# Expert result loads, a shared gating and a turn of maxima moved in a one-core FFN, attention, FFN kernel

## The chip, the cores and the metric

The kernel runs on one core of a Trainium2 chip, as one program. The metric is the device time of an execution in microseconds, and the median over several is compared. TensorE, VectorE, ScalarE, GpSimd and SyncE each run their own list of instructions in order and wait for one another through semaphores. SyncE only starts DMA transfers and waits.

## What is computed

Input are 4 sequences of 256 tokens with 512 features (float32), 1024 tokens in all. The core of the reference:

```python
x = L0_attn_hidden_states
x = x + 0.5 * _L0_ffn_ref(_layernorm(x), ...)   # router, 16 experts, shared expert
x = x + _L0_attn_ref(_layernorm(x), Wqkv, Wo)   # 32 query heads of 16, one key/value head, causal, ALiBi
x = x + 0.5 * _L0_ffn_ref(_layernorm(x), ...)   # same weights again
return x
```

The FFN sends each token to 2 of 16 experts (hidden size 128, chosen over 4 groups) and adds a shared expert (hidden size 256). An expert is `silu(x w1 + b1) * (x w2 + b2)`, then `w3`. Attention takes for each query head the softmax of scores plus a slope times the distance over the keys up to the query's own.

## The kernel before, in words

**Tiles.** The 1024 tokens are 8 tiles of 128 (`NT`), a tile on the 128 partitions. `x` stays in SBUF through all three parts. One large SBUF tensor, `arena`, is cut into named views that overlap in time. Thus `yg`, the gathered expert results of all tiles, lies over `xn` and `xnT`, the normalised tiles and their transposes: `yg[4]` to `yg[6]` lie over `xnT[0]` to `xnT[5]`, `yg[7]` over `xnT[6]` and `xnT[7]`. The views `pr`, `attn` and others of attention lie further behind.

**FFN** (`ffn_pe`, `ffn_act`, `ffn_dve`, `ffn_pool`, `ffn_sp`, called with f = 0 and f = 1). TensorE turns the tiles, does the router and the shared expert for tiles 0 to 5, then loops over 19 jobs (128 gathered token rows of one expert each). Results go to `y_dram` by scatters from GpSimd. Then come `shared_down(5)`, `shared_up(6)`, `shared_up(7)` (L1317, 16 matmuls each), and `shared_down(6)`. A `shared_down(t)` (L1358, two matmuls of 512 columns in float32, each of which the trace shows as two, and L1362, the bias matmul) waits for the gating of both tiles of its pair:

```python
pe.wait_ge(sem("s_h"), NT * f + 2 * (t // 2) + 2)
```

The gating `shared_h(t)` is one VectorE instruction (L856) behind ScalarE's silu (L632). `shared_x(t)` (L1004) adds a shared result to `x`; `pairs_x(t)` (L1014 and L1016) adds the two expert results of each token, once their load has landed.

**Loads of the expert results** (`ffn_sp`). Once all scatters have landed, SyncE issues `y_rows(range(4))`, in the first FFN the 1 MB of `wq` (into `wj`, L359), then waits for the last `shared_up` (`s_gu`) and issues `y_rows(range(4, NT))` (L355, 512 KB each), then waits for the last `shared_down` (`s_z`) and loads `wo`.

**The passage to attention** (`att_dve` L1203 and on, `att_pe`). VectorE's list is written out by hand: `pairs_x(0)`, `pairs_x(1)`, `att_stats(0)` (L1118 to L1122), `shared_h(7)`, `att_norm(0)` (L1131, two tiles, behind a reciprocal root on GpSimd, L552), `shared_x(6)`, `pairs_x(2)`, `shared_x(7)`, `pairs_x(3)`, `att_stats(1)`, and further pairs among the remainders of the q and k products (`rest`, L1150 and L1146). TensorE's list there: `shared_down(6)`, two turns of the normalised tiles (`xa_turn`, L1511), `shared_down(7)`, then the q and k products (L1522, L1530).

**Scores and maxima.** For each of 4 batches and 32 heads TensorE makes the scores (`scores`, L1551 to L1553) only to find each row's maximum; VectorE reduces them (`maxima`, L1159). The maxima are signed (`maxima_signed`, L1166 to L1168), turned by TensorE (`max_turn`, L1595), split in three bfloat16 parts by VectorE (`maxima_parts`, L1177 to L1180), written by SyncE to `m_dram` and read back as rows of `qside` (`m_rows`, L403 and L406), each for half of the heads. The scores of batch 0 are made among the q products of batches 2 and 3.

**The loop of attention.** 32 groups (4 batches of 8, q is the place in the batch). Group (b, q) holds four `scores` of batch b + 1, two `scores_t` of batch b (L1565, L1567, the turned scores with maxima), their exponentials on ScalarE (L762), a mask on GpSimd (L592), and `weigh` of the group before (L1579). The scores of batch b + 1 wait for VectorE to have reduced those two heads back. From head 16 on `scores_t` needs the second half of its batch's maxima, that is from group q = 4. For b = 1 to 3 the second turn of maxima stands inside group q = 0. For b = 0 it stands ahead of the loop: `maxima_signed(0, 1)` and `maxima_parts(0, 1)` at L1253 and L1254, `max_turn(0, 1)` at L1643, followed by a wait for the last `rest`.

Of the kernel before, what the change touches and what calls it, by code (L numbers as in the profile page):

```python
# [111 lines left out]
def build(nc, x_in, wqkv_in, wo_in, rw_in, rb_in, rbias_in, ew1, eb1, ew2, eb2, ew3, eb3,  # L112
          sw1, sb1, sw2, sb2, sw3, sb3, const_f, const_b, rows_q, rows_k, out):
    with ExitStack() as ctx:
# [5 lines left out]
        def sem(name):  # L120
            if name not in sems:
                sems[name] = ctx.enter_context(nc.semaphore(name))
            return sems[name]
# [203 lines left out]
        def ffn_sp(f):  # L327
            for t in range(NT):

                nc.sync.wait_ge(sem("xn"), NT * f + t + 1)  # L330
                nc.sync.dma_start(xn_dram[t * P:(t + 1) * P, :], xn[:, t, :]).then_inc(sem("xn_out"), 16)
            if f == 1:

                nc.sync.wait_ge(sem("a_wo"), NT)
                nc.sync.dma_start(sw3s, sw3.rearrange("(c p) d -> p c d", p=P)).then_inc(sem("wo_in"), 16)

            if f == 0:

                for e in range(0, E, EG):
                    for part in range(2):  # L340
                        if e > 0:
                            experts_in(nc.sync, e, part)
                    nc.sync.dma_start(w3[:, e:e + EG, :], ew3[e:e + EG].rearrange("e p d -> p e d")).then_inc(sem(f"ew_in{e // EG}"), 16)

            if f == 0:
                nc.sync.dma_start(wkv, wqkv_in[:, DIM:].rearrange("(c p) n -> p c n", p=P)).then_inc(sem("wqkv_in"), 16)
            nc.sync.wait_ge(sem("jex"), f + 1)
            rest = nc.sync.value_load(jm[:], min_val=JOBS_LEAST // 2 - AHEAD, max_val=JOBS // 2 - AHEAD)
            outs = nc.sync.to_reg(16 * rest + 32)
            nc.sync.wait_ge(sem(f"y_out{f}_1"), outs)  # L350
            nc.sync.wait_ge(sem(f"y_out{f}_0"), outs)
            nc.sync.wait_ge(sem("y_end"), 16 * (f + 1))
            def y_rows(tiles):
                for t in tiles:
                    nc.sync.dma_start(yg[:, t], y_dram.rearrange("(c n) d -> n c d", c=CHOICES)[t * P:(t + 1) * P]).then_inc(sem(f"yg{t}"), 16)  # L355

            y_rows(range(4))
            if f == 0:
                nc.sync.dma_start(wq, wqkv_in[:, 0:DIM].rearrange("(c p) n -> p c n", p=P)).then_inc(sem("wqkv_in"), 16)  # L359

            nc.sync.wait_ge(sem("s_gu"), NT * f + NT)
            y_rows(range(4, NT))
            if f == 0:
                nc.sync.wait_ge(sem("s_z"), NT)
                nc.sync.dma_start(wo, wo_in.rearrange("(c p) n -> p c n", p=P)).then_inc(sem("wo_in"), 16)
# [768 lines left out]
        def att_dve(pairs_x, shared_h, shared_x):  # L1134
# [27 lines left out]
            def maxima_signed(b, half):  # L1162

                hs = slice(half * HEADS // 2, (half + 1) * HEADS // 2)
                dve.wait_ge(sem("s_max"), HEADS * b + hs.stop)
                link(dve.tensor_tensor(m3[:, hs, 1], m3[:, hs, 1], m3[:, hs, 2], ALU.max))  # L1166
                dve.tensor_scalar(nm[:, 0, hs], m3[:, hs, 0], -1.0, None, ALU.mult)
                dve.tensor_scalar(nm[:, 1, hs], m3[:, hs, 1], -1.0, None, ALU.mult).then_inc(sem("m_nm"), 1)  # L1168

            def maxima_parts(b, half):  # L1170

                n = 2 * b + half
                dve.wait_ge(sem("m_t"), n + 1)
                if n >= 1:
                    dve.wait_ge(sem("m_out"), 32 * n)
                src = ps[0:QT * HEADS, m_bank(b, half), 0:P]
                link(dve.tensor_copy(mp[:, 0, :], src))  # L1177
                link(dve.tensor_tensor(mr[:], src, mp[:, 0, :], ALU.subtract))
                link(dve.tensor_copy(mp[:, 1, :], mr[:]))
                dve.tensor_tensor(mp[:, 2, :], mr[:], mp[:, 1, :], ALU.subtract).then_inc(sem("m_parts"), 1)  # L1180
# [20 lines left out]
                    dve.bn_stats(st[:, t, :], x[:, t, :]).then_inc(sem("stats"), 1)  # L1201

            pairs_x(0)  # L1203
            pairs_x(1)
            att_stats(0)
            shared_h(7)
            att_norm(0)
            shared_x(6)
            pairs_x(2)
# [28 lines left out]
            for b in (2, 3):  # L1238
                for n in range(len(ITEMS)):
# [10 lines left out]
                        values(b)  # L1250
                    if (b, n) == (3, 0):
                        maxima_signed(0, 0)
            maxima_signed(0, 1)  # L1253
            maxima_parts(0, 1)  # L1254
            for b in range(BATCH):
                more = b + 1 < BATCH
                for q in range(HEADS // 4):
                    n = 8 * b + q
                    if q == 0 and b >= 1:
                        maxima_signed(b, 1)  # L1260
                    if q == 4 and more:
                        maxima_signed(b + 1, 0)
                    if more:
                        maxima(b + 1, 4 * q, PS_S)
                        maxima(b + 1, 4 * q + 1, PS_S + 1)
                    if n >= 2:
                        normalise(n - 2)
                    if more:
                        maxima(b + 1, 4 * q + 2, PS_S)
                        maxima(b + 1, 4 * q + 3, PS_S + 1)  # L1270
                    if q == 0 and b >= 1:
                        maxima_parts(b, 1)
                    if q == 4 and more:
                        maxima_parts(b + 1, 0)
                    if q in (5, 6) and b >= 1:
                        residual(b - 1, q - 5)
                    if q == 7 and b >= 1:
                        row_stats(b - 1)
                        ln_stats(1, b - 1)
                    if b + 1 == BATCH and q in (2, 3, 4, 5):  # L1280
                        if q == 2:
                            dve.wait_ge(sem("st_done"), HEADS // 2 * b)
                        ln_rows(1, q - 2)
# [218 lines left out]
        def att_pe(shared_down):  # L1502
# [137 lines left out]
                if 1 <= b < BATCH - 1:  # L1640
                    xa_turn(b + 1, 1)
            pe.wait_ge(sem("v_in"), BATCH)
            max_turn(0, 1)  # L1643
            pe.wait_ge(sem("rest"), len(ITEMS) * BATCH)

            for b in range(BATCH):
                more = b + 1 < BATCH
                for q in range(HEADS // 4):
                    n = 8 * b + q
                    if (b, q) == (0, 0):  # L1650
                        pe.wait_ge(sem("rows1_in"), 16)
                    if (b, q) == (1, 1):
                        pe.wait_ge(sem("wo_in"), 16)
                    if (b, q) == (0, 0):
                        pe.wait_ge(sem("m_parts"), 1)
                    if more:
                        scores(b + 1, 4 * q, PS_S)
                    scores_t(b, 2 * q)
                    if more:
                        scores(b + 1, 4 * q + 1, PS_S + 1)  # L1660
                    if n >= 2:
                        if (b, q) == (0, 2):
                            pe.wait_ge(sem("m_parts"), 2)
                        if b >= 1 and q == 1:
                            pe.wait_ge(sem("m_parts"), 2 * b + 2)
                        if b >= 1 and q in (3, 4):
                            pe.wait_ge(sem("a_aT"), QT * (b - 1) + q - 2)
                        if more and q == 5:
                            pe.wait_ge(sem("m_parts"), 2 * b + 3)
                        if b >= 1 and q in (6, 7):  # L1670
                            pe.wait_ge(sem("att_x"), QT * (b - 1) + q - 5)
                        turn_back(n - 2)
                    if more:
                        scores(b + 1, 4 * q + 2, PS_S)
                    scores_t(b, 2 * q + 1)
                    if more:
                        scores(b + 1, 4 * q + 3, PS_S + 1)
                    if n == 1:
                        pe.wait_ge(sem("s_max"), HEADS)
                    if n >= 1:  # L1680
                        weigh(n - 1)
                    if q == 0 and b >= 1:
                        pe.wait_ge(sem("normed"), n - 1)
                        max_turn(b, 1)
                    if b >= 1 and q in (2, 3):
                        pe.wait_ge(sem("normed"), n - 1)
                        attn_turn(b - 1, q - 2)
                    if q == 4 and more:
                        if n >= 2:
                            pe.wait_ge(sem("normed"), n - 1)  # L1690
                        max_turn(b + 1, 0)
                    if b >= 1 and q in (5, 6):
                        pe.wait_ge(sem("normed"), n - 1)
                        out_product(b - 1, q - 5)
# [51 lines left out]
```

## Time and profile before

| | |
|---|---|
| median of 3 runs | 467.0 us (466.22 to 468.55) |
| the profiled execution | 467.78 us, span 466.0 us |
| mean granted TensorE clock | 0.97 |
| TensorE (matmul) busy | 409.6 us, 88% |
| VectorE busy | 261.9 us, 56% |
| ScalarE busy | 180.3 us, 39% |
| GpSimd busy | 162.7 us, 35% |
| first FFN, up to its last `shared_up` | 0 to 131 us |
| passage, q and k products | 131 to 201 us |
| loop of attention | 201 to 333 us |
| last FFN | 338 to 466 us |

The span runs from the first to the last instruction of the profiled execution; what lies around it is 1.8 us. Matmul time is modelled and pipelined, so neighbouring instructions overlap in the rows. The clock is a share of 2.4 GHz: 1.00 is that, 0.50 is 1.2 GHz, and a figure between is a stretch with both. "DVE" is VectorE, "ACT" ScalarE, "POOL" GpSimd, "SPq" SyncE's DMA issues. In a timeline row "[0.62 <-X]" says that the engine stood idle 0.62 us before, until X released it.

### The profile page before, as it was taken

The page shows a single profiled execution, that of the slowest core. Times are in us where ns is not written, and L with a number is a line of the kernel's source. Part 1 is how long each engine was busy: PE and PEld are TensorE (multiplying, and loading weights), DVE is VectorE, ACT ScalarE, POOL GpSimd, SP SyncE. Part 2 cuts the span into 40 slices and gives each one's busy share as a digit, 9 for nine tenths or more (in the row PEclk, how much of TensorE's full clock was granted, in tenths as well). Part 3 has the DMA queues.
Part 4 walks back from the last instruction along what each step waited for, and adds up shares of the span by engine and source line. Part 5 has one row for each costly group of instructions (what it writes and reads, how often), then busy time and mean ns, then how long its engine had stood idle before and what let it go on. Part 6 is the DMA issues. An engine that isn't in the chain of part 4 may idle for free.

```text
span 466.0 us, 8466 instructions
## 1 busy us (share of the span) xinstructions
PE 409.6 (88%) x2848; PEld 289.0 (62%) x2849; DVE 261.9 (56%) x729; ACT 180.3 (39%) x300; POOL 162.7 (35%) x230
## 2 busy tenths in 40 slices
PE   0799879999959979879999899798999879999982
PEld 1687567888636757546665465343687558888650
DVE  5489513333258955868885785633239932333347
ACT  1321235665102221146663364483522316665300
POOL 2611316665302852333332242252000054666300
PEclk9999998999979999979999999999999989999987
DMA  7999973534296479212211200020120042444277
GB/s 213 312 372 313 322 234 129 171 108 158 99 364 191 129 181 194 75 39 73 74 56 26 69 6 6 0 74 24 46 91 1 1 134 79 171 132 147 95 269 305
DMA packets 48620, 63.88 MB, mean 137 GB/s; under 512 B 7750, under 2 KB 28070, under 8 KB 48548
## 3 DMA queue, kind: packets, MB, share of 16 engines
q1 hardware_dynamic: 40220, 41.51, 28.2%
q0 software_dynamic: 6368, 19.19, 12.8%
q10 hardware_dynamic: 2000, 2.76, 2.0%
q8 instruction: 19, 0.31, 0.3%
q14 instruction: 13, 0.11, 0.1%
HBM read 46.06 MB, written 19.79 MB: 141 GB/s over the span
## 4 chain that ended last, share of the span: by engine, by line
PE 57%; DVE 15%; DMA 9%; SPq 9%; issue 5%; POOL 2%; ACT 1%; ACTq 0%; POOLq 0%; DVEq 0%
PE ps L1453 14%; PE ps L1460 7%; PE ps L1607 6%; SPq L320 5%; PE ps L1579 5%; PE ps L1438 3%; DMA w<-in_L_ffn_ew_dram 3%; PE ps L1317 3%; PE ps L1522 3%; PE ps L1551 3%; DMA q_dram<-arena 2%; DVE arena L1159 2%; PE ps L1553 2%; PE ps L1565 2%; PE ps L1589 2%
## 5 line engine op out<-in xcount | busy, mean ns | idle before, releaser
L1159 DVE TENSOR_REDUCE arena<-ps 128x3 f32<-128x384 f32 x128 | 67.2, 550 | 17.5 <-PE ps L1553 16.7
L1453 PE MATMUL ps<-arena,wj 128*128 128x128 f32 x608 | 75.5, 278 | 0.0
L1453 PEld LDWEIGHTS ps<-arena,wj 128*128 128x128 f32 x608 | 72.6, 195 | 1.0 <-issue 1.0
L762 ACT ACTIVATE arena<-ps 128x768 f32<-128x768 f32 x64 | 51.8, 811 | 50.7 <-PE ps L1567 49.8
L592 POOL TENSOR_SCALAR_AFFINE_SELECT arena<-arena 128x512 f32<-128x512 f32 x64 | 40.8, 637 | 83.3 <-ACT arena L762 82.9
L1056 DVE SCALAR_TENSOR_TENSOR arena<-ps,arena 128x128 f32<-128x128 f32 x38 | 13.3, 351 | 87.6 <-ACT arena L678 87.6
L1317 PE MATMUL ps<-arena,turns 128*128 128x256 f32 x256 | 57.6, 381 | 0.0
L1317 PEld LDWEIGHTS ps<-arena,turns 128*128 128x128 f32 x256 | 48.2, 190 | 8.1 <-issue 2.1
L524 POOL DMA_INDIRECT y_dram<-arena x38 | 38.4, 1011 | 40.1 <-DVE arena L1063 31.6
L519 POOL DMA_INDIRECT arena<-xn_dram,arena x34 | 33.2, 977 | 51.4 <-DVE arena L996 25.2
L1460 PE MATMUL ps<-w,arena 128*128 x76 | 40.1, 611 | 4.0 <-DVE arena L1056 4.0
L1551 PE MATMUL ps<-cb 128*128 128x256 bf16 x128 | 36.1, 282 | 5.0 <-DVE arena L1159 4.5
L1358 PE MATMUL ps<-turns,arena 128*128 128x512 f32 x64 | 33.7, 653 | 7.1 <-issue 7.1
L683 ACT COPY wj<-w 128x1024 f32 x38 | 39.6, 1047 | 0.0
L1553 PE MATMUL ps<-arena 116*128 116x256 bf16 x128 | 35.5, 278 | 0.0
L674 ACT COPY arena<-ps 128x512 f32<-128x512 f32 x38 | 22.3, 587 | 31.4 <-PE ps L1438 31.4
L1522 PE MATMUL ps<-arena,wj 128*128 128x256 f32 x128 | 31.6, 383 | 1.5 <-ACT arena L720 1.5
L632 ACT ACTIVATE arena<-ps,shb 128x256 f32<-128x256 f32 x16 | 7.6, 473 | 59.3 <-PE ps L1317 59.3
L1438 PEld LDWEIGHTS ps<-cf,arena 128*128 128x128 f32 x136 | 17.3, 145 | 20.3 <-issue 18.5
L1607 PE MATMUL ps<-turns,arena 128*128 128x512 f32 x64 | 29.5, 604 | 0.0
L1552 PE MATMUL ps<-arena 116*128 116x128 bf16 x128 | 28.8, 225 | 0.0
L1579 PE MATMUL ps<-arena 128*32 128x128 f32 (+1 forms) x512 | 27.8, 335 | 0.0
(190 smaller groups left out, 609.7 us busy)
## 6 DMA issues: line engine op xcount, KB each, us to landing
arena<-y_dram SPq DMA_DIRECT2D x16, 512.0 KB, 7.4
arena<-q_dram SPq DMA_DIRECT2D x36, 128.0 KB, 2.6
xn_dram<-arena SPq DMA_DIRECT2D x16, 256.0 KB, 5.8
w<-in_L_ffn_ew_dram SPq DMA_DIRECT2D x4, 1024.0 KB, 10.9
q_dram<-arena SPq DMA_DIRECT2D x16, 192.0 KB, 2.4
x<-_attn_hidden_states_dram SPq DMA_DIRECT2D x4, 512.0 KB, 6.0
out_dram<-x SPq DMA_DIRECT2D x8, 256.0 KB, 4.7
turns<-in_L_ffn_sw_dram ACTq DMA_DIRECT2D x3, 512.0 KB, 7.8
```

The source lines that it names most:

```text
L592: pool.affine_select(diagonal, diagonal, [[0, 2], [0, 2], [1, P]], ALU.is_ge, 0.0, base=0, channel_multiplier=-1).then_inc(sem("sel"), 1)
L683: act.copy(wj[:, par].rearrange("p c f -> p (c f)"), w12[:, ds(e, 1)].rearrange("p a c f -> p (a c f)")).then_inc(sem(f"wj{f}"), 1)
L762: act.activation(pr[:, n % 2, pair, :], ps[:, bank:bank + 2, :].rearrange("p a b -> p (a b)")[:, 0:768], ACT.Exp).then_inc(sem("exp"), 1)
L1159: dve.tensor_reduce(m3[:, h:h + 1, :], ps[:, bank, 0:3 * P].rearrange("p (n k) -> p n k", n=3), AX_X, ALU.max).then_inc(sem("s_max"), 1)
L1317: ins = pe.matmul(o, sw12[:, c, cols], xnT[:, 2 * pair:2 * pair + 2, c, :], start=(c == 0), stop=(c == KC - 1))
L1453: ins = pe.matmul(o, wj[:, par, c, n * INTER:(n + 1) * INTER], xgT[:, par, c, :], start=(c == 0), stop=(c == KC - 1))
L1460: pe.matmul(ps[:, PS_Y + par, :], hj[:, par, :], w3[:, ds(e, 1), :], start=True, stop=True).then_inc(sem(f"y{f}"), 1)
L1522: ins = pe.matmul(ps[:, PS_ST + c, 0:SEQ], wq[:, k, c * P:(c + 1) * P], xaT[b % 2][:, k, :], start=(k == 0), stop=(k == KC - 1))
L1551: pe.matmul(o.rearrange("p (n k) -> p n k", k=P)[:, 0:3:2, :], identb, mask, start=True, stop=True)
L1553: pe.matmul(o[:, P:3 * P], qside[0:R_MAX, p, h, P:2 * P], kT[0:R_MAX, b, :], start=False, stop=True, skip_group_check=True).then_inc(sem(" ...
L1579: ins = pe.matmul(o, vv[:, b, k, :], pr_blocks(n % 2, h // 2)[:, k * QT:(k + 1) * QT - k, h % 2, :], start=(k == 0), stop=True, skip_group ...
L1607: ins = pe.matmul(ps[:, at_bank(b, t), :], aT[t][:, c, :], wo[:, c, :], start=(c == 0), stop=(c == KC - 1))
```

## The change

Three edits. In `ffn_sp`, the loads of tiles 4 to 6 wait for the sixth `shared_up` (`s_gu` at `NT * f + NT - 2`) instead of the eighth, and only tile 7 waits for that; this holds in both FFNs. In `att_dve`, `shared_h(7)` stands ahead of `pairs_x(1)`. In the loop of attention the second turn of maxima of batch 0, with its signs and parts, stands inside group (0, 0), where the other batches have it; TensorE's wait for `normed` stays for b >= 1 alone.

```diff
--- before.py
+++ after.py
@@ -358,8 +358,10 @@
             if f == 0:
                 nc.sync.dma_start(wq, wqkv_in[:, 0:DIM].rearrange("(c p) n -> p c n", p=P)).then_inc(sem("wqkv_in"), 16)
 
+            nc.sync.wait_ge(sem("s_gu"), NT * f + NT - 2)
+            y_rows(range(4, NT - 1))
             nc.sync.wait_ge(sem("s_gu"), NT * f + NT)
-            y_rows(range(4, NT))
+            y_rows((NT - 1,))
             if f == 0:
                 nc.sync.wait_ge(sem("s_z"), NT)
                 nc.sync.dma_start(wo, wo_in.rearrange("(c p) n -> p c n", p=P)).then_inc(sem("wo_in"), 16)
@@ -1201,9 +1203,9 @@
                     dve.bn_stats(st[:, t, :], x[:, t, :]).then_inc(sem("stats"), 1)
 
             pairs_x(0)
+            shared_h(7)
             pairs_x(1)
             att_stats(0)
-            shared_h(7)
             att_norm(0)
             shared_x(6)
             pairs_x(2)
@@ -1250,13 +1252,11 @@
                         values(b)
                     if (b, n) == (3, 0):
                         maxima_signed(0, 0)
-            maxima_signed(0, 1)
-            maxima_parts(0, 1)
             for b in range(BATCH):
                 more = b + 1 < BATCH
                 for q in range(HEADS // 4):
                     n = 8 * b + q
-                    if q == 0 and b >= 1:
+                    if q == 0:
                         maxima_signed(b, 1)
                     if q == 4 and more:
                         maxima_signed(b + 1, 0)
@@ -1268,7 +1268,7 @@
                     if more:
                         maxima(b + 1, 4 * q + 2, PS_S)
                         maxima(b + 1, 4 * q + 3, PS_S + 1)
-                    if q == 0 and b >= 1:
+                    if q == 0:
                         maxima_parts(b, 1)
                     if q == 4 and more:
                         maxima_parts(b + 1, 0)
@@ -1640,7 +1640,6 @@
                 if 1 <= b < BATCH - 1:
                     xa_turn(b + 1, 1)
             pe.wait_ge(sem("v_in"), BATCH)
-            max_turn(0, 1)
             pe.wait_ge(sem("rest"), len(ITEMS) * BATCH)
 
             for b in range(BATCH):
@@ -1679,8 +1678,9 @@
                         pe.wait_ge(sem("s_max"), HEADS)
                     if n >= 1:
                         weigh(n - 1)
-                    if q == 0 and b >= 1:
-                        pe.wait_ge(sem("normed"), n - 1)
+                    if q == 0:
+                        if b >= 1:
+                            pe.wait_ge(sem("normed"), n - 1)
                         max_turn(b, 1)
                     if b >= 1 and q in (2, 3):
                         pe.wait_ge(sem("normed"), n - 1)
```

## Rows read from the trace of the kernel before

**Rows 1.** The page: granted TensorE clock in 40 slices, tenths.

```profile
PEclk9999998999979999979999999999999989999987
```

**Rows 2.** Chain that ended last, 120 to 235 us: start, us, what.

```profile
131.25 4.75 issue
136.00 3.75 PE ps L1358 x4
...
141.49 1.72 PE ps L1358 x4
```

**Rows 3.** Timeline, 128 to 144 us: start, us, engine line, [idle before <-releaser].

```profile
131.29 0.47 ACT L632 ACTIVATE arena<-ps,shb 128x256 f32<-128x256 f32 x1 [2.98 <-PE ps L1317]
132.16 0.75 DVE L1014 SCALAR_TENSOR_TENSOR x<-arena,hv,x 128x512 f32<-128x512 f32 x1 [0.62 <-DMA arena<-y_dram]
...
135.41 0.48 DVE L856 SCALAR_TENSOR_TENSOR arena<-ps,shb,arena 128x256 f32<-128x256 f32 x1
...
136.35 1.00 DVE L1131 TENSOR_SCALAR arena<-x,mv,rstd 128x512 f32<-128x512 f32 x2 [0.45 <-POOL rstd L552]
...
140.22 0.69 DVE L1004 SCALAR_TENSOR_TENSOR x<-ps,x 128x512 f32<-128x512 f32 x1 [2.87 <-PE ps L1362]
...
143.04 0.38 PE L1362 MATMUL ps<-e3x,arena 102*128 102x512 bf16 x1
...
143.46 0.69 DVE L1004 SCALAR_TENSOR_TENSOR x<-ps,x 128x512 f32<-128x512 f32 x1 [1.10 <-PE ps L1362]
```

**Rows 4.** Busy time by stretch: PE, PEld, DVE, ACT, POOL; PEclk, DMA share, GB/s.

```profile
134.00:135.00 1.00, 0.00 (x0) 0.00 (x0) 1.00 (x2) 0.00 (x0) 0.00 (x0) 0.55 0.99 338
...
140.00:141.00 1.00, 1.00 (x7) 1.00 (x6) 0.78 (x2) 0.00 (x0) 0.00 (x0) 0.53 1.04 385
...
143.50:160.00 16.50, 16.50 (x79) 12.23 (x78) 15.51 (x34) 4.55 (x12) 10.14 (x15) 1.00 0.50 141
```

**Rows 5.** Timeline, 199 to 203.3 us.

```profile
199.68 0.55 DVE L1159 TENSOR_REDUCE arena<-ps 128x3 f32<-128x384 f32 x1
...
200.92 0.16 DVE L1168 TENSOR_SCALAR arena<-arena 128x16 f32<-128x16 f32 x1
201.23 0.27 PE L1595 MATMUL ps<-cf,arena 128*64 128x128 f32 x1 [2.12 <-DVE arena L1168]
...
202.63 1.01 DVE L1159 TENSOR_REDUCE arena<-ps 128x3 f32<-128x384 f32 x2
...
203.23 0.40 PE L1551 MATMUL ps<-cb 128*128 128x256 bf16 x1 [0.73 <-DVE arena L1159]
```

**Rows 6.** Busy time by stretch, columns as in rows 4: start of attention.

```profile
203.00:209.00 6.00, 5.77 (x32) 3.56 (x36) 3.81 (x8) 2.59 (x4) 2.00 (x4) 0.50 0.06 11
209.50:212.50 3.00, 3.00 (x43) 1.91 (x36) 2.34 (x6) 1.99 (x3) 0.80 (x3) 1.00 0.00 0
```

**Rows 7.** Timeline of TensorE, 208 to 213 us.

```profile
208.46 1.19 PE L1579 MATMUL ps<-arena 128*32 128x256 f32 x16
```

**Rows 8.** DMA issues at 128.7 and 131.3 us: KB each, us to landing.

```profile
wj<-in_L_attn_Wqkv_dram SPq DMA_DIRECT2D x1, 1024.0 KB, 9.3
...
arena<-y_dram SPq DMA_DIRECT2D x1, 512.0 KB, 8.1
```

**Rows 9.** Last FFN: three stretches (columns as in rows 4), then the timeline.

```profile
450.00:451.00 1.00, 0.00 (x0) 0.00 (x0) 0.96 (x2) 0.00 (x0) 0.00 (x0) 1.00 0.98 375
452.00:453.00 1.00, 1.00 (x2) 0.48 (x3) 0.00 (x0) 0.00 (x0) 0.00 (x0) 0.50 0.64 166
453.50:463.00 9.50, 3.95 (x9) 1.34 (x7) 9.29 (x14) 0.00 (x0) 0.00 (x0) 0.86 0.96 367
...
453.24 0.75 DVE L1014 SCALAR_TENSOR_TENSOR x<-arena,hv,x 128x512 f32<-128x512 f32 x1 [1.59 <-DMA arena<-y_dram]
```

**Rows 10.** Timeline of SyncE, 200 to 216 us.

```profile
204.63 0.58 SPq L406 DMA_DIRECT2D arena<-m_dram  x2
214.44 1.87 SPq L389 DMA_DIRECT2D arena<-q_dram  x3
```

## The prediction

> **What bounds the kernel now.** I read the page first: TensorE's granted clock is near full except in a few of the 40 slices [rows 1]. One of these is the twelfth, 128 to 140 us, and the chain, read there in order of time, shows why: TensorE runs out of work at 131.25, stands for 4.75 us with nothing that the profile can name, and then does a shared down product (L1358, four matmuls) in 3.75 us, where the same four take 1.72 us a moment later [rows 2]. So that pause costs its length, and then a half-speed product.
>
> The timeline says what it waits for [rows 3]. `shared_down(6)` needs `shared_h(7)`. ScalarE has its input ready at 131.76 (131.29 + 0.47), but VectorE takes it in program order behind `pairs_x(1)` and `att_stats(0)`, at 135.41. TensorE starts 0.11 us after it ends (135.89 to 136.00). Then `shared_x(6)` waits 2.87 us for the product, and `shared_x(7)` comes at 143.46. From 143.5 to 160 VectorE is busy for 15.51 of 16.5 us [rows 4]: it bounds the stage that follows, and what it gains at 143.46 it keeps. The clock falls to 1.2 GHz (0.50) in 134 to 135, is there until shortly before 141 and then at 2.4 GHz (1.00) [rows 4].
>
> The same kind of place lies at the start of attention [rows 5]. VectorE's last maxima of the first batch begin at 199.68, `maxima_signed(0, 1)` ends at 201.08, and TensorE, without work since about 199.1, turns the maxima at 201.23, with 2.12 us of idle before it. Then VectorE splits them (201.50 to 202.63), and only then takes the first reduction of the next batch. TensorE has done two score products and waits for that: next matmul at 203.23. The clock is at 0.50 from 203 to 209; from 209.5 it is full [rows 6]. The first `weigh`, which closes group 1, ends at 209.65 [rows 7].
>
> **The loads (edit 1).** Tiles 4 to 6 of the expert results no longer wait for the last shared product. In the first FFN SyncE would issue them at 129.3 to 130.8 and not from 131.28; each issue is some 0.5 us. But the DMA engines are already full: their share is 0.99 at 134 to 135 and 1.04 at 140 to 141 [rows 4], the weights issued at 128.73 land only 9.3 us later, at 138.0, and tile 4, issued at 131.28, 8.1 us later, at 139.4 [rows 8]. The transfers land in the order of issue, one behind the other; a load put into the full queue sooner lands no sooner. Nor does one wait for it: `pairs_x(4)` is behind all of the work of rows 3. In the last FFN the queue is as full when tile 4 is issued (share 0.98 at 450 to 451), the wait that counts is the 1.59 us before `pairs_x(2)`, whose load isn't moved, and from 453.5 to 463 VectorE is busy for 9.29 of 9.5 us [rows 9]. I take 0. Bounds: a gain of 0.5 us, should the gap in the transfers at 452 to 453 (share 0.64 [rows 9]) come from the late issue; a loss of 0.5 us, should tile 7's issue stand one slot later. Past `wqkv`'s load nothing is moved, since the three loads come after it; its cover is 138.0 against the first q product at 143.4, and this shrinks to 2 us below.
>
> **`shared_h(7)` one place up (edit 2).** `pairs_x(0)` ends at 131.54 (132.16 less its idle of 0.62). `shared_h(7)` then runs at 131.8 to 132.28, mostly in the idle time before `pairs_x(1)`, which is pushed from 132.16 to 132.3: 0.14 us, carried through `att_stats(0)` to the reciprocal root on GpSimd, for which `att_norm(0)` waits [rows 3]. Before, `shared_h(7)` lay under that wait (0.45 us of it are left in the row), so it cost VectorE nothing there; now the cover is the wait for a load, and if this went it would cost up to its 0.48 us. `att_norm(0)` begins at 136.49 instead of 136.35, its two halves done at 137.0 and 137.5. TensorE starts `shared_down(6)` at 132.39 and, still at full clock, needs 2.1 us (1.72 for the four matmuls [rows 2] and 0.38 for the bias [rows 3]), to 134.5. Then it waits for `att_norm(0)` up to 137.1. What is next late is thus this normalisation. Upper bound of the gain: at full clock the two turns end at 137.9 and `shared_down(7)` at 140.0, `shared_x(7)` stands at 140.05, 3.4 us early. Lower bound: clock at half from 137: two turns to 138.4 (1.3 us, from 140.2 to 141.49, where the next product began [rows 2, 3]), the down product with its bias 4.2 us as from 136.00 to 140.2, where `shared_x(6)` began [rows 3], `shared_x(7)` at 142.6, 0.9 us early. Here stands an idle time of 2.6 us after 2.1 us of work. The nearest row is the other pause: 2.12 us after dense work, and the clock was down within 1.8 us of its end [rows 5, 6]. So I expect a fall, but a late one that takes a part of the stage: the middle, **2.2 us**.
>
> The Trainium skill (TensorE: Matmul & The Clock Gate, Part 1, on oscillation) lets the clock fall only after a pause longer than 2.12 or 2.6 us. This trace doesn't agree: its fall at 203 follows a pause of 2.12 us [rows 5, 6]. By the rule the clock would hold in this stage, and the term be the upper bound, 3.4 us.
>
> **The second turn of maxima (edit 3).** Nothing is removed: one transpose, three instructions of signs and four of parts all stay. TensorE's first scores of the next batch no longer stand behind the turn. They need the last maxima (199.68 + 0.55), so they start at 200.35, not 201.46: 1.1 us. VectorE goes from the signs (201.08) straight to the reductions of group 0, a pair each 1.01 us [rows 5]: 201.1 to 203.3 with a small wait for the scores; the parts follow, 1.1 us, to 204.4; then four more, of which the second lets the last score product of group 1 go: 205.45, and `weigh(0)` runs 205.9 to 206.7. Before, group 1 ended at 209.65, 2.95 us later; I take **2.8 us** if the clock holds. 0.5 us of it is the wait for the turn that is now hidden, the rest the half speed that is not paid and the place of the parts behind group 0's products. TensorE's pauses are then 1.25 us and a few under 1.4 us, shorter than each pause after which the rows show a fall. If the clock falls all the same, 1.1 us (the earlier start) is left. The wait that moves is TensorE's for `maxima_signed`: behind it stood all of group 0, now group 1's scores, when it has long been met. The maxima's own round trip through memory is later by 1.8 us; its second half was issued at 204.63, its reader is a product of group 4 at about 215.4 (209.65 and two groups of 2.9), and SyncE's next work starts at 214.44 [rows 10]: hidden, with a cover of some 7 us.
>
> **Sum.** The profiled execution took 467.78 us, 0.8 above the median of 467.0. 467.78 less 2.2, 2.8 and 0 is 462.8. Some runs at the median may have lost less to the clock and then have less to win, so I don't take the 0.8 off as well: **462.9 us**, and the rivals stand against 467.78 too. What a measurement can tell from no change is about 0.5%, 2.3 us; faster means under 464.7.
>
> **Rivals.** A is the forecast, 0.46.
>
> B: the clock holds at both places. 467.78 less 3.4 and 2.8: 461.6 us. For it: no pause above 2.6 us is left there. Against it: the fall after 2.12 us. 0.14. The skill's rule quoted above comes out here.
>
> C: the first gain is absorbed. The start of attention is paced by something that edit 2 doesn't move, such as the weights' landing at 138.0 or the round trip of q through memory. Against it: VectorE's 15.51 of 16.5 us behind it. Only 2.8 is left: 465.0. 0.15.
>
> D: the clock falls again in groups 0 and 1. 2.2 and 1.1 us off: 464.5. 0.13.
>
> E, slower: the parts now stand between groups 0 and 1, so that TensorE pauses for some 1.3 us at 203.7 to 205, and the fall comes not in groups paced by VectorE but in the dense ones, 2 and later (3.00 of 3.00 us busy at 209.5 to 212.5 [rows 6]), where each us at half clock costs half a us. The spells at half clock here last near 7 us [rows 4, 6]; two of them cost 6.8 us. Less the 2.8 and the least of edit 2, 0.9, that is 3.1 slower: 470.9. It decides once more than 7.4 us behind 205 run at half clock. 0.06.
>
> F: neither stall is on the way to the end, and the time is 467.0. Against it: the chain runs through both. 0.06.
>
> **How the numbers follow.** Range: from B's time less 1.4, for runs that lie 0.8 lower as the median did and loads that gain 0.5, to C's and 0.6 for loads that lose: 460.2 to 465.6. Outside are E, F and tails. Faster: nearly all of A, B, half of D, a quarter of C: 0.70. Slower: E, 0.06. The same: 0.24.
>
> **What would show it.** Edit 2: no idle of 4.75 us before L1358 but one near 1.1, and one of 2.6 before L1511; `shared_x(7)` at 140 to 142.5. If it is at 143, edit 2 failed. Edit 3: L1595 behind four score products, the second group of `weigh` ending some 7.6 us after the last maxima of batch 0 and not 9.9; clock at 1.00 there. Edit 1: tile 4 lands at 139.4 all the same, with a longer time from issue to landing. Wrong would be: a stage behind 160 us that gives the early start back, or half clock in groups 2 to 4.

## The result, and the profile after

The changed kernel takes 463.68 us (median of 20 runs, 458.89 to 465.42), the kernel before 467.55 us (median of 20 runs of the same comparison). The ratio is 0.9922, with a 95% interval of 0.99 to 0.9945: clear of 1, and under 1%. Each ratio here is the comparison's own and not the quotient of the medians; the two can differ by 0.3% (edit 2 alone, below: 0.9918, and 0.9949 from the medians). One execution of the kernel before in the last of the comparisons below, of 2291.56 us, was in a slower state and is in no ratio. The forecast was 462.9 us, in a range of 460.2 to 465.6. The profiled execution took 463.63 us, against 467.78 us before.

The page of the changed kernel, for [rows 1] and the table:

```profile
span 461.9 us, 8466 instructions
PE 411.6 (89%) x2848; PEld 289.2 (63%) x2849; DVE 260.0 (56%) x729; ACT 180.6 (39%) x300; POOL 163.5 (35%) x230
...
PEclk9999998999998989999999999999999979999997
```

Busy time has hardly moved, the clock row has. From here on, lines of the file behind `ffn_sp` and before L1253 are two higher in the changed kernel (the gating is L858, `shared_x` L1006, `pairs_x` L1016 and L1018, the maxima L1161); those of TensorE are as before.

The passage, timeline of the changed kernel, for [rows 3]:

```profile
131.79 0.48 DVE L858 SCALAR_TENSOR_TENSOR arena<-ps,shb,arena 128x256 f32<-128x256 f32 x1
...
132.37 1.96 PE L1358 MATMUL ps<-turns,arena 128*128 128x512 f32 x4 [1.13 <-issue]
...
137.06 1.07 PE L1511 MATMUL ps<-cf,arena 128*128 128x128 f32 x8 [2.52 <-DVE arena L1133]
...
137.97 3.38 PE L1358 MATMUL ps<-turns,arena 128*128 128x512 f32 x4
...
141.80 0.69 DVE L1006 SCALAR_TENSOR_TENSOR x<-ps,x 128x512 f32<-128x512 f32 x1 [2.38 <-PE ps L1362]
```

`shared_h(7)` runs at 131.79, TensorE is idle for 1.13 us and not 4.75, and the pause has moved: 2.52 us now stand before the turn of the normalised tiles. `shared_down(7)` takes 3.38 us for its four matmuls, which is half speed, and `shared_x(7)` starts at 141.80, 1.66 us before that of [rows 3].

Busy time by stretch in the changed kernel (columns as in [rows 4]):

```profile
134.00:135.00 1.00, 0.55 (x2) 0.00 (x0) 1.00 (x2) 0.00 (x0) 0.00 (x0) 1.00 0.99 350
138.30:141.50 3.20, 3.20 (x5) 1.16 (x4) 1.09 (x2) 0.51 (x2) 0.00 (x0) 0.50 1.05 390
165.60:168.80 3.20, 3.20 (x14) 2.20 (x12) 0.56 (x1) 0.37 (x1) 0.82 (x2) 0.50 0.79 183
199.00:205.00 6.00, 4.82 (x50) 2.85 (x49) 5.38 (x14) 3.33 (x5) 2.36 (x5) 1.00 0.14 40
298.70:302.00 3.30, 3.30 (x30) 1.35 (x23) 1.15 (x3) 2.28 (x4) 1.94 (x3) 0.50 0.06 11
```

The clock now holds at 134 to 135, where it had fallen [rows 4], but falls at about 138, in the passage; again at 165.5, at 298.6, and later in the last FFN. At 199 to 205, the place of [rows 6], it is full.

The start of attention, for [rows 5] and [rows 7]:

```profile
197.83 0.55 DVE L1161 TENSOR_REDUCE arena<-ps 128x3 f32<-128x384 f32 x1
...
198.63 0.27 PE L1551 MATMUL ps<-cb 128*128 128x256 bf16 x1 [1.36 <-DVE arena L1161]
...
199.16 2.25 DVE L1161 TENSOR_REDUCE arena<-ps 128x3 f32<-128x384 f32 x4
...
201.33 0.27 DVE L1179 CAST arena<-ps 64x128 bf16<-64x128 f32 x1
...
203.01 0.28 PE L1551 MATMUL ps<-cb 128*128 128x256 bf16 x1 [1.09 <-DVE arena L1161]
...
204.00 0.86 PE L1579 MATMUL ps<-arena 128*32 128x256 f32 x16
```

From the start of the last maxima to the end of the first `weigh` it took 9.97 us before (199.68 to 209.65) and takes 7.03 now (197.83 to 204.86). TensorE starts the scores after 1.36 us of idle, VectorE does four reductions in a row, then the parts (L1179), and TensorE's wait for the reduction behind them is the 1.09 us at 203.01.

To see where the time went, each instruction of the new trace is set against its twin, the same instruction in the old one. The new kernel is ahead by

| at (us of the trace before) | ahead by | what changed there |
|---|---|---|
| 143.5, `shared_x(7)` | 1.66 | edit 2 |
| 170 to 184 (TensorE) | 0.02 | half clock from 165.5, which the old execution didn't have |
| 199.7, last maxima of batch 0 | 1.85 | the store of q that both wait for landed 1.8 us sooner |
| 209.7, end of the first `weigh` | 4.8 | edit 3 |
| 306 to 370 | 3.5 | half clock from 298.6 |
| 442, last scatter | 3.2 | half clock once more at 370 |
| 466, end | 4.1 | tile 2 landed sooner behind the last scatter |

The third line of this table is a wait of ScalarE for a store of q, in the timeline of the changed kernel and then in that of the kernel before:

```profile
184.66 0.37 ACT L738 CAST arena<-ps 128x256 bf16<-128x256 f32 x1 [2.81 <-DMA q_dram<-arena]
```

```profile
186.50 0.87 ACT L736 CAST arena<-ps 128x256 bf16<-128x256 f32 x2 [4.64 <-DMA q_dram<-arena]
```

The stores were issued by SyncE at these times, in the same order:

```profile
178.52 1.26 SPq L381 DMA_DIRECT2D q_dram<-arena  x2
```

```profile
180.52 1.29 SPq L379 DMA_DIRECT2D q_dram<-arena  x2
```

So the lead of edit 2 wasn't lost at 165.5. TensorE lost it there, but SyncE kept it: its store of q is issued 2.0 us sooner and lands 6.1 us later instead of 5.9, and behind that wait the other engines have the lead back. The half clock at 165.5 cost nothing at the last maxima.

### The profile page after: what moved, and what is told of

It is laid out like the page before. It is cut to its first block, busy times and chain, and to the rows that moved or that the text cites. A ratio compares the mean times of both kernels' runs of the same rounds, so it can differ in the third digit from the quotient of the medians.

```text
span 461.9 us, 8466 instructions
## 1 busy us (share of the span) xinstructions
PE 411.6 (89%) x2848; PEld 289.2 (63%) x2849; DVE 260.0 (56%) x729; ACT 180.6 (39%) x300; POOL 163.5 (35%) x230
## 4 chain that ended last, share of the span: by engine, by line
PE 59%; DVE 17%; SPq 8%; DMA 8%; issue 4%; POOL 2%; ACT 1%; ACTq 0%; POOLq 0%; DVEq 0%
PE ps L1453 14%; PE ps L1460 7%; PE ps L1607 6%; SPq L320 5%; PE ps L1579 5%; PE ps L1522 4%; PE ps L1438 3%; DMA w<-in_L_ffn_ew_dram 3%; PE ps L1551 3%; PE ps L1317 3%; DVE arena L1161 2%; PE ps L1553 2%; PE ps L1565 2%; PE ps L1589 2%; SPq L343 2%
## 5 line engine op out<-in xcount | busy, mean ns | idle before, releaser
L1161 DVE TENSOR_REDUCE arena<-ps 128x3 f32<-128x384 f32 x128 | 67.3, 551 | 16.9 <-PE ps L1553 15.9
L1453 PE MATMUL ps<-arena,wj 128*128 128x128 f32 x608 | 76.5, 280 | 0.0
L1453 PEld LDWEIGHTS ps<-arena,wj 128*128 128x128 f32 x608 | 73.6, 197 | 1.0 <-issue 1.0
L1358 PE MATMUL ps<-turns,arena 128*128 128x512 f32 x64 | 34.9, 674 | 3.5 <-issue 3.5
L1522 PE MATMUL ps<-arena,wj 128*128 128x256 f32 x128 | 32.7, 393 | 1.5 <-ACT arena L722 1.5
L1607 PE MATMUL ps<-turns,arena 128*128 128x512 f32 x64 | 29.5, 604 | 0.0
```

Of the source, the lines that this page charges most:

```text
L1161: dve.tensor_reduce(m3[:, h:h + 1, :], ps[:, bank, 0:3 * P].rearrange("p (n k) -> p n k", n=3), AX_X, ALU.max).then_inc(sem("s_max"), 1)
L1453: ins = pe.matmul(o, wj[:, par, c, n * INTER:(n + 1) * INTER], xgT[:, par, c, :], start=(c == 0), stop=(c == KC - 1))
L1522: ins = pe.matmul(ps[:, PS_ST + c, 0:SEQ], wq[:, k, c * P:(c + 1) * P], xaT[b % 2][:, k, :], start=(k == 0), stop=(k == KC - 1))
L1607: ins = pe.matmul(ps[:, at_bank(b, t), :], aT[t][:, c, :], wo[:, c, :], start=(c == 0), stop=(c == KC - 1))
```

## The experiments

Eleven runs were made, of ten kernels (the changed one again among them), each timed beside the kernel before on its chip. They fall into three comparisons, and the kernel before had medians of 466.74, 466.44 and 467.66 us in them; a ratio is always to the one of its own comparison.

### Each edit alone

**Edit 1 alone** (the diff of `ffn_sp`).

> The kernel before with edit 1 alone (tiles 4 to 6 of the expert results issued behind the sixth shared up product). My theory: the DMA engines are full, the loads land one behind the other in the order of issue, so tile 4 lands at 139.4 to 140.3 in the first FFN as before though issued 2 us sooner, and the time is that of before within 0.5 us, 467 to 468. Rival: the profile of the changed kernel ended 1.1 us sooner behind its last scatter (22.9 us against 23.9) because of this edit; then this run is 0.7 to 1.1 us faster than before, and its last scatter to end is near 22.9.

467.83 us; ratio 1.0014 (0.9984 to 1.0044). Tile 4 in the first FFN was issued at 127.5, and its row of the DMA issues (KB, us to landing) is

```profile
arena<-y_dram SPq DMA_DIRECT2D x1, 512.0 KB, 10.4
```

so it landed at 137.9, 15.7 us behind the last scatter's start at 122.2. Before, that was 139.4 less 124.0, 15.4 us. Issued 2 us sooner, landed no sooner, as in a full queue. Over all profiles it is 14.7 to 16.7 us in the six without edit 1 and 15.1 to 16.4 in the seven with it. The rival's short end, 23.0 us from last scatter to the end, did come (461.9 less 439.0 is 22.9 in the changed kernel). But two kernels without edit 1, edit 3 alone and the kernel before with a filled pause (below), ended after 23.0 and 22.9 us too. The long end of the profile before, 23.9, was tile 2, which landed late in that execution.

**Edit 2 alone** (the diff of `att_dve`'s first list).

> The kernel before with edit 2 alone (shared_h(7) ahead of pairs_x(1)). My theory: the pause of 4.75 us before shared_down(6) becomes 1.1 us, shared_x(7) starts at 140.1 to 142.6 (143.46 before), and what is won there, 0.9 to 3.4 us, reaches the end: 464.1 to 466.6, the likeliest 465.4. Rival: the gain is absorbed between 160 and 200 us by the round trips of q through memory; then the last maxima of batch 0 start at 199.7 as before and the time is that of before within 0.5 us.

464.36 us; ratio 0.9918 (0.9885 to 0.9951). Timeline:

```profile
132.20 1.96 PE L1358 MATMUL ps<-turns,arena 128*128 128x512 f32 x4 [1.13 <-issue]
...
136.89 1.06 PE L1511 MATMUL ps<-cf,arena 128*128 128x128 f32 x8 [2.52 <-DVE arena L1131]
...
137.79 1.88 PE L1358 MATMUL ps<-turns,arena 128*128 128x512 f32 x4
...
139.93 0.69 DVE L1004 SCALAR_TENSOR_TENSOR x<-ps,x 128x512 f32<-128x512 f32 x1 [0.68 <-PE ps L1362]
```

Here the clock held over the same pause of 2.52 us, `shared_down(7)` took 1.88 us, and `shared_x(7)` began at 139.93. Measured from the last scatter of the first FFN that is 3.4 us sooner than before (16.1 us behind it, against 19.5), the upper bound of the prediction; in the changed kernel it was 1.66. Busy time by stretch of the same run:

```profile
134.00:138.00 4.00, 1.48 (x11) 1.13 (x10) 3.08 (x9) 0.45 (x1) 0.72 (x1) 1.00 1.04 391
163.00:168.00 5.00, 4.92 (x16) 3.58 (x17) 0.60 (x3) 0.40 (x2) 1.72 (x4) 0.50 0.75 175
201.00:206.00 5.00, 5.00 (x24) 3.13 (x24) 3.12 (x6) 1.85 (x3) 1.88 (x3) 0.50 0.05 10
```

The clock then fell in the next stage, at 163 to 168, and again at 201 to 206, since the turn is still in its old place: of the 3.5 us ahead at 160, TensorE had 0.3 left at 175 and 2.3 at the last maxima. SyncE was still 3.0 us ahead at 180. So the rival of a full absorption falls, and that of a partial one has something to it, by way of the clock and of the wait for q.

**Edit 3 alone** (the diff of the loop and of L1253, L1254, L1643).

> The kernel before with edit 3 alone (the second turn of maxima of batch 0 in group 0). My theory: from the start of the last maxima of batch 0 to the end of the first weigh it takes 7.0 to 7.7 us and not 10.0, with the clock at 1.00, and the median is 2 to 2.8 us under before, 464.7 to 465.5. Rival: without edit 2 the clock still falls there in most executions, since the pause of 1.3 us remains; then 8.5 to 9 us, and about 1 us under before.

464.21 us; ratio 0.9945 (0.992 to 0.9971).

```profile
200.38 0.55 DVE L1159 TENSOR_REDUCE arena<-ps 128x3 f32<-128x384 f32 x1
...
205.56 0.28 PE L1549 MATMUL ps<-cb 128*128 128x256 bf16 x1 [1.09 <-DVE arena L1159]
...
206.55 0.86 PE L1577 MATMUL ps<-arena 128*32 128x256 f32 x16
```

200.38 to 207.41 is 7.03 us, as in the whole change, at full clock, without edit 2 (TensorE's lines are two lower in this kernel: L1549 is the scores, L1577 `weigh`). In all six profiles of kernels that have edit 3 as written, this interval was 7.02 or 7.03 us. Its rival is out.

**Edits 2 and 3 without edit 1**, run twice, the second time beside the whole change.

> Edits 2 and 3 without edit 1. My theory: edit 1 is worth nothing, so this is as fast as the whole change, 3.5 to 4 us under before: 463.5 to 464.1. Rival: edit 1 is worth about 1 us at the end of the last FFN; then 464.6 to 465.

> Edits 2 and 3 without edit 1, again, for the comparison with the whole change on one chip. Theory: equal to it or up to 0.8 us slower, with a wait before pairs_x(4) of the last FFN. Rival: about 1 us faster than the whole change.

> The changed kernel again, all three edits, beside the next run on the same chip. Theory: edit 1 is worth 0 to 0.8 us, since in the last FFN VectorE takes tile 4 right behind tile 3 here, while with the late issue it waited 0.5 to 0.85 us for it in three profiles of four. Then this is 0 to 0.8 us faster than edits 2 and 3 without it. Rival, from the first comparisons (0.9922 against 0.9896 of before, on different chips): edit 1 costs about 1 us; then it is slower by that.

462.09 us, ratio 0.9896 (0.9862 to 0.9929) at first; then 465.37 us, 0.9949 (0.9916 to 0.9982), beside 464.43 us, 0.9949 (0.9914 to 0.9984) of the whole change. Edit 1 can't be told from nothing in the time.

The profile of the whole change run again differs from the first one in the passage:

```profile
137.05 1.06 PE L1511 MATMUL ps<-cf,arena 128*128 128x128 f32 x8 [2.52 <-DVE arena L1133]
...
137.95 1.88 PE L1358 MATMUL ps<-turns,arena 128*128 128x512 f32 x4
```

The pause is the same 2.52 us, and the clock held behind it.

In the last FFN the trace shows something, though. In the first of the runs without it, tile 4 was issued at 446.08, and VectorE waited for it:

```profile
arena<-y_dram SPq DMA_DIRECT2D x1, 512.0 KB, 6.4
```

```profile
450.21 0.75 DVE L1014 SCALAR_TENSOR_TENSOR x<-arena,hv,x 128x512 f32<-128x512 f32 x1
...
452.52 0.75 DVE L1014 SCALAR_TENSOR_TENSOR x<-arena,hv,x 128x512 f32<-128x512 f32 x1 [0.77 <-DMA arena<-y_dram]
```

In the changed kernel it was issued at 443.72:

```profile
arena<-y_dram SPq DMA_DIRECT2D x1, 512.0 KB, 7.9
```

It landed 12.7 us behind the last scatter's start (443.72 + 7.9 less 438.95), against 13.7 us in the run without (446.08 + 6.4 less 438.78). The wait for tile 4, 0.77 us here, was 0.59 in edit 2 alone and 0.38 in the filled pause; there was none in the kernel before, in edit 3 alone and in the second run of edits 2 and 3 (three waits in six profiles, not the three in four that the expectation counted). In none of the seven profiles with edit 1 does VectorE wait for tile 4. But the landings of tile 4 overlap, 12.4 to 13.6 us behind the last scatter's start with edit 1 and 12.6 to 13.7 without, and so do the ends, 22.6 to 24.5 us behind it with edit 1 and 22.8 to 23.9 without. So a wait goes in some executions, and a sooner end is not shown.

### Is edit 3's gain the clock, or the order?

The kernel before, with TensorE kept at work in the pause:

```diff
             pe.wait_ge(sem("v_in"), BATCH)
+            for _ in range(16):
+                pe.matmul(ps[:, PS_A, 2 * P:4 * P], identb, cb[:, 0:2 * P], start=True, stop=True)
             max_turn(0, 1)
```

> The kernel before with 16 matmuls of 256 columns in bfloat16 (never read, some 1.8 us) in the pause of 2.12 us before the second turn of maxima; nothing else changed, so the order of the work stays. Theory 1, the gain of edit 3 is the clock: last maxima to the end of the first weigh takes about 7.5 us instead of 10.0, and the median is 1.5 to 2.3 us under before. Theory 2, the gain is the order (TensorE's earlier start and the hidden turn): the interval stays above 9 us, and the time is within 0.7 us of before.

464.88 us; ratio 0.9971 (0.9948 to 0.9994).

```profile
197.98 0.55 DVE L1159 TENSOR_REDUCE arena<-ps 128x3 f32<-128x384 f32 x1
...
199.44 0.30 PE L1595 MATMUL ps<-cf,arena 128*64 128x128 f32 x1 [0.28 <-DVE arena L1168]
...
204.66 0.86 PE L1579 MATMUL ps<-arena 128*32 128x256 f32 x16
```

```profile
200.00:205.50 5.50, 4.63 (x47) 2.61 (x46) 5.01 (x12) 3.25 (x4) 2.05 (x4) 1.00 0.18 48
```

The order is the old one, the turn still waits for the signs, yet the interval is 197.98 to 205.52, 7.54 us. Of the 2.94 us that edit 3 takes off the profile, 2.43 are the half clock that isn't there, and 0.51 the order. Theory 1 holds for the interval. The median gains less, 1.6 us, than the 2.4 of the profile; the profile of edit 1 alone shows why: its old order took 8.44 us there, since its spell at half clock was half as long. The pause doesn't cost every execution the same. In the time of all executions the filling brought about half of what edit 3 alone did (0.9971 against 0.9945, intervals that overlap), not four fifths.

### Is the loss in the passage the clock?

The changed kernel with TensorE at work in the moved pause:

```diff
             pe.wait_ge(sem("s_x"), NT - 2)
+            for _ in range(5):
+                pe.matmul(ps[:, PS_GU, 0:2 * P], sw12[:, 0, 0:P], sw12[:, 0, 0:2 * P], start=True, stop=True)
```

> The changed kernel with five matmuls of 256 columns in float32 (results never read, some 2.2 us) on TensorE between shared_down(6) and the turn of the normalised tiles, where it stands idle 2.52 us. My theory: the pause is what lets the clock fall to 0.50 at about 138 in the profile of the changed kernel; with it filled, shared_down(7) takes 1.9 us and not 3.4, shared_x(7) starts at 140.1 instead of 141.8, and the median is about 1.2 to 1.7 us under the changed kernel (462 to 462.5). Rival: the loss of clock there isn't on the way to the end, or comes from elsewhere; then shared_x(7) may be early but the time is that of the changed kernel within 0.5 us, or 0.2 us more for the added work.

461.94 us; ratio 0.9902 (0.9868 to 0.9936).

```profile
134.02 2.32 PE L1506 MATMUL ps<-turns 128*128 128x256 f32 x10
136.61 1.11 PE L1513 MATMUL ps<-cf,arena 128*128 128x128 f32 x8 [0.27 <-DVE arena L1133]
...
137.56 1.88 PE L1358 MATMUL ps<-turns,arena 128*128 128x512 f32 x4
...
139.69 0.69 DVE L1006 SCALAR_TENSOR_TENSOR x<-ps,x 128x512 f32<-128x512 f32 x1 [0.64 <-PE ps L1362]
```

```profile
134.00:141.00 7.00, 6.74 (x31) 4.81 (x30) 5.41 (x12) 1.07 (x2) 0.72 (x1) 1.00 1.03 388
185.20:188.20 3.00, 3.00 (x11) 1.06 (x9) 2.04 (x7) 0.00 (x0) 1.06 (x2) 0.50 0.00 0
```

The five matmuls (L1506 here, the turn is L1513) end 0.27 us before the turn is released. `shared_down(7)` takes 1.88 us, `shared_x(7)` begins at 139.69, 16.1 us behind the last scatter's start (17.8 in the changed kernel). So the half speed there was the pause's doing, and that part of the rival is out. Whether the gain reaches the end is less clear: the clock is at 0.50 at 185.2 to 188.2 instead, behind the wait for q, and the lead over the kernel before shrinks from 4.4 us at 180 to 2.8 at the last maxima. The ratio is lower than that of the whole change in both of its comparisons, but the intervals overlap.

### The parts one group on

```diff
-                    if q == 0:
+                    if q == (1 if b == 0 else 0):
                         maxima_parts(b, 1)
```

> The changed kernel with maxima_parts(0, 1) behind the maxima of group 1 instead of group 0. My theory: TensorE's wait of 1.09 us inside group 1 goes (it stood behind the parts), the first weigh ends about 6.0 us after the start of the last maxima instead of 7.0, of which the turning back in group 2 gives a part back, as it waits for the parts: 0.3 to 0.9 us under the changed kernel. Rival: VectorE paces these groups, so all of it comes back in group 2, and the time is that of the changed kernel within 0.3 us.

462.30 us; ratio 0.9905 (0.9871 to 0.9939).

```profile
198.46 0.55 DVE L1161 TENSOR_REDUCE arena<-ps 128x3 f32<-128x384 f32 x1
...
203.58 0.86 PE L1579 MATMUL ps<-arena 128*32 128x256 f32 x16
...
206.83 0.86 PE L1579 MATMUL ps<-arena 128*32 128x256 f32 x16
```

The first `weigh` ends 5.98 us after the start of the last maxima (198.46 to 204.44), 1.05 us sooner than in the changed kernel. The second ends after 9.23 us instead of 9.91, so 0.37 of the 1.05 is given back in group 2 and 0.68 kept, as expected.

**All of it, with a third filled pause.** Three more such matmuls stand before the second turn of batch 2.

> The changed kernel with the five matmuls of the passage, three more of the same kind before the second turn of batch 2 (where TensorE pauses 1.57 us at 162 us and the clock fell in the profile of the changed kernel), and the parts one group on. My theory: the gains add: 1.5 to 3 us under the changed kernel, 460.7 to 462.2. Rival: the added work lies in the way in executions whose clock held anyway, and the time is that of the passage's filling alone.

463.40 us; ratio 0.9926 (0.9892 to 0.996): a miss. The profile has both gains, 16.1 us to `shared_x(7)` and 5.98 us to `weigh`, and the third filling kept the clock at 1.00 from 162 to 169. But between 180 and 190 it lost 2.6 us more than the filled passage did:

```profile
184.18 0.87 ACT L738 CAST arena<-ps 128x256 bf16<-128x256 f32 x2 [6.29 <-DMA q_dram<-arena]
```

```profile
186.50:192.50 6.00, 5.59 (x18) 2.10 (x19) 3.24 (x9) 0.28 (x2) 1.06 (x2) 0.50 0.03 6
```

ScalarE waited 6.29 us for q's store. It was 4.0 us ahead of the kernel before when the wait began (177.89 against 181.86) and 2.3 when it ended (184.18 against 186.50), and then TensorE ran at half clock for 6 us, which took the rest. The wait was longer because the work before it came 4.0 us sooner and the store landed only 2.3 us sooner, though issued 3.9 us sooner (176.65 against 180.52).

**Without the third filling:**

> The changed kernel with the filled pause of the passage and the parts one group on, without the three matmuls before the second turn of batch 2. Theory: shared_x(7) 16.1 us behind the last gather or scatter of the first FFN in every execution, first weigh 6.0 us behind the last maxima, and 1 to 2 us under the changed kernel on the same chip. Rival: what the start of attention wins is taken back at the wait for q through memory (183 to 186 us), and the time is that of the changed kernel within 0.7 us.

463.24 us; ratio 0.9892 (0.9842 to 0.9942), beside the whole change's 0.9949. This is the lowest ratio of all; its interval overlaps the others, so that it beats the changed kernel is not shown. Its profile has 16.1 us to `shared_x(7)` and 5.98 us to `weigh`.

## Why the prediction was right

**Sum.** 2.2 + 2.8 + 0 = 5.0 us were forecast against the profiled execution, 4.15 us came. The sum's terms at their own places came to 1.66 and 2.94; what lies between 4.6 and 4.15 are spells at half clock elsewhere, less a sooner end. The median moved by 3.9 us. That the time came within 0.8 us of the forecast is in part luck. Alone, edit 2 took 3.8 us off by its ratio and edit 3 took 2.6, which would add to 6.4; together they took 4.9 and 2.4 us without edit 1, and 3.6 and 2.4 with it. The intervals are 1.0 to 1.7 us to either side, so whether the gains add is not shown, and the sum took it for granted.

**Edit 1: 0 in the first FFN, right and shown** (landed no sooner). In the last FFN I put a gain of 0.5 us in the bounds. A wait for tile 4 of up to 0.77 us is there in some executions without edit 1 and in none with it, but neither the end nor the time shows a gain, so nothing here speaks against the 0. The row that I took for the proof, 1.59 us of wait for tile 2, was a late transfer of that execution; in the changed kernel tile 2's wait is 0.46 us.

**Edit 2: mechanism right in the passage.** Pause of 1.13 us (1.1 forecast), next late is the normalisation (2.52, 2.6 forecast), bounds of 0.9 and 3.4 us: both outcomes of the mechanism were met, 1.66 with a fall of the clock (at about 138 and not 137, hence not 0.9) and 3.4 without, three profiles each where the pause wasn't filled. The 2.2 is the middle of the bounds; no profile stands there, and that it is close to the mean of the two outcomes, 2.5, is luck. The 0.14 us for `pairs_x(1)` was 0.03, the tile being there. One step was too simple: "what it gains at 143.46 it keeps". VectorE does bound the stage up to 160, but then the store of q decides who waits at 184 to 186. In the changed kernel's profile the 1.66 us arrived whole, by way of SyncE; a gain of 3.4 us did not always.

**Edit 3: right in size, 2.94 against 2.8, and in its shape** (7.03 us where the working gave 206.7 less 199.68, 7.0; the 7.6 us among the prediction's signs doesn't follow from that working. The wait inside group 1 is 1.09 us for 1.3). Its division was right too: 0.5 for the hidden turn; the filled pause measures 0.51 for all of the order. That the half clock makes the rest had only been argued in the prediction and is now shown for the stage.

**The skill's rule.** The Trainium skill (TensorE: Matmul & The Clock Gate, Part 1, on oscillation) lets the clock fall only after pauses longer than these. The runs disagree: after the same pause of 2.52 us, the clock fell in the changed kernel and in both runs of edits 2 and 3, and held in edit 2 alone, with the parts one group on, and in the second run of the whole change. Neither the rule nor my own reading of [rows 5, 6] (a pause of 2.12 us, so it falls) describes that; a chance would have been the right form.

**Rivals.** D is out: in none of the nine profiles with edit 3 did the clock fall in groups 0 and 1. E is out with it: it didn't fall in groups 2 to 4 either. F is out: edits 2 and 3 alone each came out clear of 1. B, the clock holding at both places, came in the profile of the second run of the whole change (`shared_x(7)` 16.1 us behind the last scatter, 7.02 us to `weigh`), so it is not another outcome but some executions of this kernel. That execution took 463.39 us and not B's 461.6, with half clock at 163, 296 and 374 us and a later end. C is half right: the start of attention does stand behind the round trip of q, but edit 2 moves that trip too.

**Left open:** why the clock holds over one pause of 2.52 us and falls over the next; and how much of a gain in the passage the wait for q takes back on average. Measured from the last scatter against the kernel before, 1.66 us at `shared_x(7)` were 1.5 to 1.9 at the last maxima, in three profiles. 3.4 us were 3.3 in one and 1.8 to 2.8 in four, and with the third filling nothing was left. Part of that is the profile compared with: three others without edit 2 lost 0.6 to 1.1 us on the same stretch, and that of the kernel before stands for one execution. Nothing was tried against E beyond reading the clock there.

## What to carry to other kernels

When a pause of TensorE stands before dense work, try to fill or shorten the pause: here four fifths of what a moved transpose gained in its stage was the half clock behind the pause, and matmuls that nobody reads brought those four fifths without any reordering. Then look at the next wait: a third filling kept the clock and gained nothing, as the store of q had not come sooner by as much. A lead can travel on another engine than the one that you watch, here SyncE. A load issued 2 us sooner into a full DMA queue landed no sooner; see whether its row of time to landing just grows by what the issue moved (10.4 us for 8.1). And when a single profiled execution shows a wait, look for it in a second one before it carries a term.

## What was not expected of the hardware

The same instructions, the same pause of 2.52 us, and TensorE at 1.2 GHz in one execution of the changed kernel and 2.4 GHz in another: 3.38 against 1.88 us for four matmuls of 512 columns in float32. Spells at half clock also came at places that no edit touches, at 165.5 and 298.6 us in the changed kernel, each of which cost TensorE 1.3 to 1.7 us at once. The one at 165.5 lay ahead of the wait for q and cost nothing behind it. In five other profiles TensorE came to that wait without such a spell, and one stood behind it, at 185 to 190 us, where it took some 1.5 us or more of TensorE's lead. Executions of one kernel spread over some 5 to 6 us, more than any one edit is worth here. Over the 20 of the changed kernel the time falls as the mean clock rises, with a correlation of -0.67, so the clock explains under half of that spread, and the rest is not explained. A change of this size needs several runs, and a trace must be read stage by stage and not by its end.
